# Half-width exponentials in an attention loop, with one normalisation step moved and one semaphore token split

## The reference

```
xn   = layernorm(x)
Q, K = poincare_fully_connected(xn, z_q, b_q), poincare_fully_connected(xn, z_k, b_k)
V    = xn @ w_v.T + b_v
x    = x + layernorm(softmax(Q K^T / 8) V)           # 16 heads of 64
xn   = layernorm(x);  xp = xn shifted by one row
xr   = mu_r*xn + (1-mu_r)*xp;  xk = mu_k*xn + (1-mu_k)*xp
x    = x + layernorm(sigmoid(xr W_r^T) * (relu(xk W_k^T)^2 W_v^T))
```

## Time and profile before

| | us |
|---|---|
| median of 3 runs (range) | 4590.73 (4571.56 to 4593.59) |
| the profiled execution's own time | 4600.45 |
| its span (slowest core, 7) | 4598.9 |
| spans of the eight cores | 4568.4 to 4598.9 |
| mean granted TensorE clock, core 7 | 0.63 of 2.4 GHz |
| busy: PE / VectorE / ScalarE | 2316.2 / 1454.4 / 1597.0 |

### The profile page before, as it was taken

How to read it: one execution, slowest core, us unless ns; L and a number is a source line. 1 busy time by engine, 2 the same in 40 slices (tenths; PEclk the granted TensorE clock), 3 DMA queues, 4 the chain that set the end, 5 groups by cost and what they waited for, 6 DMA issues and landing times.

```text
span 4598.9 us, 25867 instructions; the slowest of 8 cores (4568.4 to 4598.9 us)
## 1 busy us (share of the span) xinstructions
PE 2316.2 (50%) x7360; PEld 629.8 (14%) x7360; DVE 1454.4 (32%) x2455; ACT 1597.0 (35%) x1209; POOL 162.1 (4%) x256
## 2 busy tenths in 40 slices
PE   0634415555655565573316533255556557556613
PEld 0211101111211121120102111011112112111101
DVE  2444430003313313322534544200133243142154
ACT  0245443333333333332103345333333333334311
POOL 0000110000000000000000000000000000000000
PEclk9866755555665565575657667555557557556657
DMA  6211133111112202201051211511120220122010
GB/s 109 68 32 38 31 76 59 41 41 41 39 30 68 50 20 59 59 23 35 19 128 37 55 37 28 94 40 31 41 54 16 67 60 21 30 68 50 20 46 28
DMA packets 325773, 216.98 MB, mean 47 GB/s; under 512 B 276224, under 2 KB 284544, under 8 KB 325632
## 3 DMA queue, kind: packets, MB, share of 16 engines
q1 hardware_dynamic: 287488, 109.87, 10.7%
q0 software_dynamic: 38144, 105.45, 9.4%
HBM read 169.03 MB, written 42.21 MB: 46 GB/s over the span
## 4 chain that ended last, share of the span: by engine, by line
PE 45%; ACT 29%; DVE 12%; issue 6%; DMA 5%; SPq 1%; ACTq 1%; DVEq 1%; POOL 0%; POOLq 0%
ACT pool L1092 19%; PE p_attA L1037 12%; PE psc L1068 10%; PE p_attB L1045 9%; PE psc L646 3%; PE psc L937 2%; PE psc L681 2%; PE psc L917 2%; ACT pool L508 1%; ACT pool L537 1%; ACT pool L511 1%; ACT pool L540 1%; PE p_attB L646 1%; PE p_attA L646 1%; DMA pool<-x 1%
## 5 line engine op out<-in xcount | busy, mean ns | idle before, releaser
L1092 ACT ACTIVATE pool<-psc 128x2048 bf16<-128x2048 f32 x512 | 961.0, 1877 | 1858.9 <-PE psc L1075 1858.9
L1037 PE MATMUL p_attA<-pool 128*65 128x512 bf16 x1024 | 596.7, 583 | 1138.8 <-ACT pool L1092 995.7
L1099 DVE CAST pool<-p_attA 1x512 bf16<-1x512 f32 x64 | 43.8, 685 | 1966.9 <-PE p_attB L1045 1928.4
L1068 PE MATMUL psc<-pool 64*128 64x512 bf16 x1024 | 581.8, 580 | 80.3 <-DMA pool<-s_vaug 80.3
L1045 PE MATMUL p_attB<-pool 128*65 128x512 bf16 x1024 | 605.7, 591 | 0.0
L1075 PE MATMUL psc<-pool 64*128 64x512 bf16 x1024 | 581.9, 580 | 0.0
L1037 PEld LDWEIGHTS p_attA<-pool 128*65 128x65 bf16 x1024 | 132.5, 129 | 1593.6 <-issue 1592.3
L461 PE MATMUL psc<-dump,ones_bf 128*128 128x512 bf16 x64 | 35.7, 585 | 431.6 <-DVE dump L455 431.6
L681 PE MATMUL psc<-w_sb,pool 128*128 128x512 bf16 x512 | 154.8, 471 | 174.3 <-DVE pool L696 172.7
L896 PE MATMUL psc<-pool,w_sb 128*128 128x512 bf16 x512 | 129.6, 408 | 217.1 <-DVE smc L884 208.1
L1068 PEld LDWEIGHTS psc<-pool 64*128 64x128 bf16 x1024 | 97.0, 100 | 789.9 <-issue 789.9
(11 more groups left out here) (128 smaller groups left out, 2338.8 us busy)
## 6 DMA issues: line engine op xcount, KB each, us to landing
pool<-s_vaug SPq DMA_DIRECT2D x64, 520.0 KB, 4.3
pool<-s_kfm SPq DMA_DIRECT2D x64, 512.0 KB, 3.3
pool<-x POOLq DMA_DIRECT2D x8, 2048.0 KB, 9.1
pool<-x POOLq DMA_DIRECT2D x32, 512.0 KB, 4.5
out<-pool POOLq DMA_DIRECT2D x32, 512.0 KB, 2.9
s_vaug<-pool POOLq DMA_DIRECT2D x32, 260.0 KB, 2.3
s_qfm<-pool POOLq DMA_DIRECT2D x32, 256.0 KB, 4.2
s_kfm<-pool POOLq DMA_DIRECT2D x32, 256.0 KB, 4.4
```

Of the source, the lines that this page charges most:

```text
L1037: T(lambda t, c=c, po=po, vof=vof: t.matmul(p_attA[0:65, :], vsl[:, vof:vof + 65], PT[:, po:po + 512], start=(c == 0), stop=(c == 15), ski ...
L1068: T(lambda t, kof=kof, qof=qof, reg=reg: t.matmul(psc[:, reg:reg + 512], Ksl[0:64, kof:kof + 128], Qsl[0:64, qof:qof + QB], start=True, st ...
L1092: lambda s, po=po: s.activation(PT[:, po:po + 2048], psc[:, 0:2048], AF.Exp, scale=0.125),
```

## The change

Three edits, none of which changes what is computed.

1. The exponential is made chunk by chunk, 1024 columns in and out, instead of once per two chunks. It is emitted after PV of the chunk before. Its slot in `PT` is c % 4; it waits for its own chunk's scores and for PV of chunk c-4.
2. `emit_bndA_v` is emitted ahead of pair 0's loop instead of after pair 0's hand-over, so that it stands before the hand-over in VectorE's queue. In the tail nothing moves.
3. In `emit_bndD` the corrections of xr come directly after its mix, before the xk mix, and give a token of their own, `cy["mix_r"]`; R's matmuls wait for that one, K's still for `cy["mix"]`. The instructions are the same.

```diff
--- before.py
+++ after.py
@@ -744,7 +744,8 @@
             "exp": {}, "pvg": {}, "rc": None, "dn": None, "ofx": None,
             "afm_free": [None, None], "x1stt": None, "x1ntm_free": None,
             "x2c": [None, None],
-            "mix": None, "v2": None, "ffn_pu": [None, None],
+            "mix": None, "mix_r": None, "v2": None,
+            "ffn_pu": [None, None],
             "of_free": None, "odma": [None, None], "rfree": None,
             "kafree": None, "xrkfree": None,
         }
@@ -847,9 +848,12 @@
             if bnd["qb"] == 0:
                 V(lambda v: v.memzero(smcol("x1prev")), inc=1)
             x1n4 = x1n_fm.rearrange("p (tt c i) -> p tt c i", tt=4, c=NCH)
+            dv8 = dump.bitcast(F32)[:, 0:8]
+            dv24 = dump.bitcast(F32)[:, 8:32].rearrange(
+                "p (a b) -> p a b", a=3)
             tk_mix = None
-            for dst, mu, mum1 in [(xr_fm, "mur", "murm1"),
-                                  (xk_fm, "muk", "mukm1")]:
+            for dst, mu, mum1, key in [(xr_fm, "mur", "murm1", "mix_r"),
+                                       (xk_fm, "muk", "mukm1", "mix")]:
                 d4 = dst.rearrange("p (tt c i) -> p tt c i", tt=4, c=NCH)
                 for ci in range(NCH):
                     V(lambda v, d4=d4, mu=mu, ci=ci: v.tensor_scalar(
@@ -864,11 +868,6 @@
                         smcol(mum1, ci),
                         d4[:, :, ci:ci + 1, 1:128].squeeze(2),
                         ALU.mult, ALU.add), inc=1)
-            dv8 = dump.bitcast(F32)[:, 0:8]
-            dv24 = dump.bitcast(F32)[:, 8:32].rearrange(
-                "p (a b) -> p a b", a=3)
-            for dst, mum1 in [(xr_fm, "murm1"), (xk_fm, "mukm1")]:
-                d4 = dst.rearrange("p (tt c i) -> p tt c i", tt=4, c=NCH)
                 b0 = d4[:, 0:1, :, 0:1].squeeze(3).squeeze(1)
                 V(lambda v, mum1=mum1: v.tensor_mul(
                     dv8, smcol("x1prev"), smcol(mum1)), inc=1)
@@ -880,6 +879,7 @@
                 b3 = d4[:, 1:4, :, 0:1].squeeze(3)
                 tk_mix = V(lambda v, b3=b3: v.tensor_add(b3, dv24, b3),
                            inc=1)
+                cy[key] = tk_mix
             prevsrc = x1n4[:, 3:4, :, 127:128].squeeze(3).squeeze(1)
             tk_mix = V(lambda v: v.tensor_copy(smcol("x1prev"), prevsrc),
                        waits=[tk_mix], inc=1)
@@ -899,7 +899,7 @@
                         fchunk(xr_fm, ci),
                         start=(ci == 0), stop=(ci == NCH - 1),
                         skip_group_check=True),
-                        waits=[cy["mix"], tk_wset, pu[dc % 2]],
+                        waits=[cy["mix_r"], tk_wset, pu[dc % 2]],
                         inc=(1 if ci == NCH - 1 else 0))
                 tk_e = Sc(lambda s, dc=dc: s.activation(
                     sgE[:], p_ff[dc % 2], AF.Exp, scale=-1.0),
@@ -1054,6 +1054,7 @@
             for pr in range(8):
                 if pr == 0 and pend_b is not None:
                     emit_bndA_y(pend_b)
+                    emit_bndA_v(pend_b)
                 sl = pr % 2
                 for c in range(16):
                     reg = (c % 2) * 1024
@@ -1080,21 +1081,20 @@
                         inc=1)
                     if c == 15:
                         tk_qkl[pr] = tk_qk
-                    if c % 2 == 1:
-                        if c >= 4:
-                            wslot = tk_pvg.get((pr, c - 3))
-                        elif pr >= 1:
-                            wslot = tk_pvg.get((pr - 1, 12 + c))
-                        else:
-                            wslot = cy["pvg"].get(12 + c)
-                        po = ((c // 2) % 2) * 2048
-                        tk_exp[(pr, c)] = tk_exp[(pr, c - 1)] = Sc(
-                            lambda s, po=po: s.activation(
-                                PT[:, po:po + 2048], psc[:, 0:2048],
-                                AF.Exp, scale=0.125),
-                            waits=[tk_qk, wslot], inc=1)
                     if c >= 1:
                         emit_pv(pr, c - 1)
+                    if c >= 4:
+                        wslot = tk_pvg.get((pr, c - 4))
+                    elif pr >= 1:
+                        wslot = tk_pvg.get((pr - 1, 12 + c))
+                    else:
+                        wslot = cy["pvg"].get(12 + c)
+                    po = (c % 4) * 1024
+                    tk_exp[(pr, c)] = Sc(
+                        lambda s, reg=reg, po=po: s.activation(
+                            PT[:, po:po + 1024], psc[:, reg:reg + 1024],
+                            AF.Exp, scale=0.125),
+                        waits=[tk_qk, wslot], inc=1)
                 emit_pv(pr, 15)
                 V(lambda v: v.tensor_copy(rcb[0:1, 0:QB],
                                           p_attA[64:65, :]),
@@ -1120,9 +1120,7 @@
                     bnd_cur["x2t"][0] = emit_x2q(qb, 0, cy["x2c"][0])
                     bnd_cur["x2t"][1] = emit_x2q(qb, 1, cy["x2c"][1])
                 if pend_b is not None:
-                    if pr == 0:
-                        emit_bndA_v(pend_b)
-                    elif pr == 1:
+                    if pr == 1:
                         emit_bndB(pend_b)
                     elif pr == 2:
                         emit_bndC(pend_b)
```

## The result

The changed kernel takes 3493.05 us (median of 10 runs, 3489.49 to 3530.44) against 4583.91 before in the same comparison: ratio 0.7632, 95% interval 0.7613 to 0.7651. The forecast was 3490, range 3410 to 3620. The ratio is that of the means, without executions such as the one of 3530.44 us, in which the cores of one die took over 1% longer than the other's at a lower granted clock. The profiled execution took 3518.84 us, 26 more than the median; its span is 3517.3 on core 7, the other cores lie between 3479.3 and 3516.3.

What follows compares the result with a forecast made beforehand. TensorE and ScalarE were taken to alternate without overlap, at 1.2 GHz, 5.29 us per two chunks. Savings 869 - 16 + 12 + 81 + 130 + 24 = 1100 from 4600.45 leave 3500, 3490 for the median; range 3410 to 3620.

Steps and rivals of the forecast that it cites:

- Both limits: Per chunk at 2.4 GHz: the loop through exponential, PV and scores at 1.12 us, ScalarE alone at 1.11; 1.13 taken.
- The term of 1.0 us: Plain pairs: 4 us at 1.2 GHz after each hand-over, costing 1.0 us a pair.
- Rival 1: Attention: TensorE's clock doesn't rise or doesn't stay up, plain pairs take 27.3 us, total 3770; chance 8%.
- Rival 2: Attention: the clock rises to 0.81 only, a chunk takes 1.22 us, 78 us more, total 3568; chance 16%.
- Term 117: Pair 0 of later query blocks: the second edit loses 22.8 x 4 + 13.0 x 2 = 117 us of the first's gain.
- Rival 3: Pair 0: the moved step costs nothing as its transposes land earlier than in the tail; 117 less, 3373; chance 4%.
- Pair 2: `emit_bndB` and the copies behind it make this pair 27.4 us; 13.5 saved, 6 times, 81 us.
- The tails: After attention, R starts 12.0 us sooner through the third edit and K doesn't wait; twice, 24 us saved.
- The term for the third edit beside attention: After pair 4 with `emit_ffn1`: without this edit R would start some 5 us later in each.
- Loads: K, Q and V of a pair, asked for one pair ahead: DMA has room at twice the rate, nothing added.
- Rival 4: Attention chunks: the split exponential doesn't overlap, 2.84 us a chunk against 2.64, total 4796; chance 2%.
- Rival 5: Attention chunks: part of the loop is slower, 1.2 to 1.35 us a chunk, 60 to 190 us more; chance 10%.

Runs made afterwards that it cites:

- experiment 5: Experiment 1's kernel plus 12 extra matmuls of unused constants after each pair's first two scores: 3345.47 us, ratio 0.7297.
- Experiment 8: The 3375 us kernel (edits 1 and 3) with two exponentials of 512 columns per chunk: 3562.04 us, ratio 0.7787.
- experiment 4: The kernel before plus 8 extra matmuls of unused constants in each wait for an exponential: 4024.28 us, ratio 0.8801.
- experiment 1: The changed kernel without the second edit, so the first layernorm's step stays behind pair 0's hand-over: 3375.07 us, ratio 0.7354.
- experiment 3: The kernel before with only the second edit, the moved first layernorm step: 4622.5 us, ratio 1.0068.
- experiment 11: Experiment 1's kernel without the third edit's token, so R waits for the whole mix again: 3443.75 us, ratio 0.7508.
- edit 3 alone: The kernel before with only the third edit, R waiting just for the corrections of xr: 4555.14 us, ratio 0.9931.

## Why the prediction was right, point by point

*One chunk.* Half exponential 1.02, measured 1.024. Chunk 1.13, measured 1.12 to 1.13 at 2.4 GHz; experiment 5 shows it in whole pairs, 16.8 / 15. Both limits were real and as near each other as said: ScalarE's row has no gaps but the 0.09 between instructions, and TensorE waits 0.20 of every 1.12 us. Experiment 8 shows the ScalarE side by lengthening it.

*The clock.* It rises inside pairs and stays. This was argued from the pauses; experiment 4 shows it: filling the pauses alone lifted the clock from 0.51 to 1.00. That it falls after a hand-over is shown by experiment 5. The term of 1.0 us was somewhat small: on core 7 chunk 0 to chunk 15 takes 18.1 on average in plain pairs, 1.3 more than the 16.8 without the fall. Rival 1 is out.

*Rival 2, the 0.81 clock.* It came, but on a part of the cores and of the time. Core 7 shows 0.82 in the window 695 to 850 against 0.89 in 2430 to 2600. There a pair of exponentials, ScalarE's rows:

```profile
706.42 2.14 ACT L1094 ACTIVATE pool<-psc 128x1024 bf16<-128x1024 f32 x2 [0.24 <-PE psc L1076]
708.81 2.14 ACT L1094 ACTIVATE pool<-psc 128x1024 bf16<-128x1024 f32 x2 [0.24 <-PE psc L1076]
```

starts every 2.39 us, so a chunk is 1.19, where the rival had 1.22. The dies' medians are 3483.9 and 3509.3 us at a mean of 0.793 and 0.778, so it explains a good part of 25 us between dies in this execution. The one pair 4 of 72.4 us has the same clock in its `emit_ffn1` stretch:

```profile
1029.00:1080.00 51.00, 46.09 (x177) 15.71 (x177) 13.14 (x22) 16.38 (x16) 0.00 (x0) 0.81 0.02 6
```

It doesn't hold over the run, as the rival's 78 us had it. In the trace's clock records cores 0 to 3 have no stretch at 0.81 at all, cores 4 to 7 have 318 to 390 us of some 3500. The Trainium skill ("TensorE: Matmul & The Clock Gate", Part 1, "Seeing it yourself") says that three cores of a die in dense matmuls take it to 13/16 of its clock, and that it stays there while the load lasts. This trace agrees with the level. It doesn't agree with its staying, for all eight cores do the same work, unless this work isn't dense in the page's sense, which no run here shows.

*The moved step.* Term 117, measured 118 by experiment 1; pair 0 of 44.8 and 35.0 measured 45.0 to 45.5 and 34.4 to 35.4. Rival 3 is out: the DMA wait is 13.05 us, as in the tail before. The remark that 41 us had covered all but 4 of it was measured as about 5 by experiment 3.

*VectorE's blocks.* Pair 2: 27.4, measured 26.4 to 27.0. `emit_ffn1`: 66.3, measured 66.7 to 67.4 and once 72.4. The tails: 12.0 each, measured 12.7. The term for the third edit beside attention, 5 us each, was 2 short (experiment 11, 7 each): I had counted the wait and not the slow matmuls behind it.

*What was missed.* Loads were said to leave room. At the start of the first sequence's attention they didn't: TensorE waits for pair 1's first loads.

```profile
722.77 0.58 PE L1069 MATMUL psc<-pool 64*128 64x512 bf16 x1 [6.22 <-DMA pool<-s_vaug]
```

These 6.22 us were hidden before, when pair 0 took 41; pair 0 there is 27.9 on core 7. On other cores the same pair takes 21.7 to 30.6 us, in either sequence, so this term, put at nothing, was worth 0 to 9 us each time.

*The sum.* That it was right to 3 us (3490 against 3493) is partly luck. In the profiled executions core 7 saved 4598.9 - 3517.3 = 1082 us where 1100 were forecast. Term by term, forecast in brackets: plain pairs 860 (869), pair 0 of the later blocks -3 (-4), pair 2 86 (81), pair 4 120 (130, and 6 of the 10 are the one pair at the 0.81 clock), tails 25 (24), the first loads -6 (0). In medians 1091 were saved, 9 short; the kernel before was 7 faster in the comparison (4583.91) than in the three runs that the forecast started from (4590.73), and that leaves the 3.

Rival 4 isn't borne out anywhere. Rival 5 neither: the exponential is on the line, and the only longer chunks are those at a lower clock (1.19 at 0.81, 1.53 at 1.2 GHz).

*Left open.* What the overlap would give with the clock held low was not measured; the rows at 1.2 GHz after a hand-over give 1.53 a chunk, for two to four chunks of a pair only. The cause of the time that edit 3 alone saved beyond 25 us, if it is real, isn't known.

## What to carry to other kernels

When one engine's instruction covers both buffers of a pair that another engine fills, that engine has nothing to fill during it. Cutting it at the buffer's border gives overlap as long as the fixed part (0.17 us here) stays small beside the piece. It can lift TensorE's clock on top: filling the pauses alone gave 8.7 of the 18.7 us that a plain pair gained here. Once the main loop is half as long, everything that had been placed in its shadow must be counted again: a step in front of a waited-for copy cost 20 us before and 118 after. A stretch of the old trace in which the same side work runs alone (here the tail) gives its length in the new kernel closely: 44.8 us were read there, 45.0 to 45.5 came.

## What was not expected of the hardware

Matmuls that nobody needs, 4096 of them, took the old kernel to 0.8801 of its time, with nothing else changed; that they would help was forecast before experiment 4, at 470 us, and 565 came. And a copy out of PSUM costs VectorE 0.69 us for 512 columns whether it moves 1, 64 or 65 partitions, so that taking the denominators along was free.
